# A graph layer's correction rows written into PSUM by ScalarE and accumulated onto by TensorE, in place of an addition on VectorE

## What is computed

```python
N_NODES = x.shape[0]
agg  = segment_sum(x[src], dst)              # sum of the neighbours' rows
deg  = segment_sum(ones, dst)
mean = agg / maximum(deg, 1)
h    = mean @ W_l + b + x @ W_r
y    = x + silu(h)
out  = (y - mean(y)) / sqrt(var(y) + 1e-5)   # along each row
```

## Time and profile before

| | us |
|---|---|
| median of 3 runs (1616.44 to 1617.76) | 1617.12 |
| the profiled execution's own time | 1616.76 |
| its span in the trace | 1615.0 |
| PE busy | 1574.8 (98%) |
| DVE busy | 1408.7 (87%) |
| ACT busy | 1028.8 (64%) |
| POOL busy | 947.9 (59%) |
| DMA, mean rate | 217 GB/s |

### The profile page before, as it was taken

How to read it: one execution, slowest core, us unless ns; L and a number is a source line. 1 busy time by engine, 2 the same in 40 slices (tenths; PEclk the granted TensorE clock), 3 DMA queues, 4 the chain that set the end, 5 groups by cost and what they waited for, 6 DMA issues and landing times.

```text
span 1615.0 us, 24709 instructions
## 1 busy us (share of the span) xinstructions
PE 1574.8 (98%) x7886; PEld 1311.1 (81%) x7886; DVE 1408.7 (87%) x2174; ACT 1028.8 (64%) x1433; POOL 947.9 (59%) x1089
## 2 busy tenths in 40 slices
PE   7998899999999999999999999999999999999996
PEld 5887688888888888888888888888888888888884
DVE  7988799999996888888888888888888888888886
ACT  4443343333335777777777777777777777777775
POOL 6446566666654665655566556665556656666563
PEclk9999999999999999999999999999999999999998
DMA  5456589888884676766667666666667666677674
GB/s 186 147 163 189 170 262 266 263 265 262 266 250 150 220 230 201 237 211 216 223 208 227 218 213 219 219 221 213 222 212 228 217 210 231 205 228 221 205 235 152
DMA packets 204245, 350.52 MB, mean 217 GB/s; under 512 B 37020, under 2 KB 51126, under 8 KB 204117
## 3 DMA queue, kind: packets, MB, share of 16 engines
q1 hardware_dynamic: 156135, 274.22, 51.6%
q0 software_dynamic: 46944, 74.22, 16.7%
q10 hardware_dynamic: 1038, 0.50, 0.1%
HBM read 288.78 MB, written 139.67 MB: 265 GB/s over the span
## 4 chain that ended last, share of the span: by engine, by line
PE 95%; DVE 2%; DMA 1%; issue 1%; SPq 0%; ACT 0%; POOL 0%; POOLq 0%; DVEq 0%
PE pH L473 81%; PE pT L567 9%; PE pT L541 3%; PE pT L482 1%; DMA light_h<-in_x 0%; DVE w_sum L799 0%; DVE w_sum L794 0%; DVE sums L923 0%; DMA light_x<-in_x 0%; PE pH L500 0%; PE pH L503 0%; DVE stats L1001 0%; SPq L246 0%; DVE row_mask L790 0%; DVE Z L794 0%
## 5 line engine op out<-in xcount | busy, mean ns | idle before, releaser
L473 PE MATMUL pH<-ws_hi,x_hi 128*128 128x512 f32 x1564 | 629.1, 402 | 0.0
L473 PE MATMUL pH<-ws_hi,x_lo 128*128 128x512 f32 x1564 | 611.4, 391 | 0.0
L473 PE MATMUL pH<-ws_lo,x_hi 128*128 128x512 f32 x1564 | 609.4, 390 | 0.0
L383 POOL DMA_INDIRECT cor<-correction_rows,node_idx x347 | 366.2, 1055 | 313.3 <-ACT cor L671 229.8
L708 ACT ACTIVATE x_hi<-pT 128x1024 fp32r<-128x1024 f32 x174 | 178.1, 1024 | 272.7 <-PE pT L567 272.7
L473 PEld LDWEIGHTS pH<-ws_hi,x_lo 128*128 128x128 f32 x1564 | 293.6, 188 | 63.3
L473 PEld LDWEIGHTS pH<-ws_lo,x_hi 128*128 128x128 f32 x1564 | 294.7, 188 | 54.5
L473 PEld LDWEIGHTS pH<-ws_hi,x_hi 128*128 128x128 f32 x1564 | 294.2, 188 | 54.5 <-issue 0.3
L986 DVE TENSOR_TENSOR Z<-pH,cor 128x1024 f32<-128x1024 f32 x174 | 212.5, 1221 | 100.4 <-PE pH L473 94.6
L717 ACT ACTIVATE O<-Z,shift,rstd 128x512 f32<-128x512 f32 x347 | 261.9, 804 | 3.2 <-DVE shift L1011 3.2
L1001 DVE BATCH_NORM_STATS2 stats<-Z 128x6 f32<-128x512 f32 x347 | 221.4, 680 | 0.0
(11 more groups left out here) (132 smaller groups left out, 1785.6 us busy)
## 6 DMA issues: line engine op xcount, KB each, us to landing
X<-in_x SPq DMA_DIRECT2D x173, 512.0 KB, 4.2
out<-O SPq DMA_DIRECT2D x173, 512.0 KB, 5.1
correction_rows<-c_out SPq DMA_DIRECT2D x98, 256.0 KB, 4.2
light_x<-in_x SPq DMA_DIRECT2D x66, 256.0 KB, 5.0
light_h<-early_product SPq DMA_DIRECT2D x44, 256.0 KB, 5.7
out<-light_o SPq DMA_DIRECT2D x44, 256.0 KB, 5.5
join_row<-joined SPq DMA_DIRECT2D x98, 64.0 KB, 4.1
light_h<-in_x SPq DMA_DIRECT2D x22, 256.0 KB, 2.9
```

The lines of the kernel that those rows point to most:

```text
L383: g.indirect_dma_start(out=out_, out_offset=None, in_=table, in_offset=bass.IndirectOffsetOnAxis(ap=idx, axis=0), bounds_check=bound, oob_ ...
L473: last = mm(ps, a[:, k], w[:, k], start=(n == 0), stop=(n == len(terms) - 1))
```

## The change

ACT gets a new step, `seed`: it copies the pair's correction rows `cor` into the two banks of `pH`. PE's matmuls of the pair wait for that (`seeded`) and accumulate from the first on, so `pH` holds the whole of h afterwards. Silu then reads `pH` and writes `Z`. `add_cor` on DVE and its semaphore are gone. ACT's order becomes silu t-1, `round_x` t+1, seed t+1, `reset_cor` t+3, light, normalise t-3. The reset of a third `cor` buffer joins the two in the edge stage, and POOL gathers for three pairs before `serve`, then for t+3 in turn t. One matmul more, written to the second bank of `pH[1]` after the edge tiles (`banks_open`), makes that bank ready for accumulation; its values are written over. For pairs 0 and 1 the seed waits for the last two edge tiles' `finish` and for `banks_open`, in place of PE's wait for `finish`.

```diff
--- before.py
+++ after.py
@@ -165,11 +165,12 @@
         c_stored = [sem(f"c_stored{b}") for b in range(2)]
         x_in = [sem(f"x_in{b}") for b in range(4)]
         cor_in = [sem(f"cor_in{b}") for b in range(4)]
-        transposed, hi_made, lo_made, product, z_made, silu_made = (sem("transposed"), sem("hi_made"), sem("lo_made"),
-                                                                   sem("product"), sem("z_made"), sem("silu_made"))
+        transposed, hi_made, lo_made, product, silu_made = (sem("transposed"), sem("hi_made"), sem("lo_made"),
+                                                                   sem("product"), sem("silu_made"))
         u_made, stats_made, mv_made, eps_added, rstd_made, shift_made, normed = (
             sem("u_made"), sem("stats_made"), sem("mv_made"), sem("eps_added"), sem("rstd_made"),
             sem("shift_made"), sem("normed"))
+        seeded, banks_open = sem("seeded"), sem("banks_open")
         cor_reset = sem("cor_reset")
         stored = [sem(f"stored{b}") for b in range(2)]
 
@@ -448,9 +449,10 @@
             gather_light(0)
             single(0, gather_cor)
             single(1, gather_cor)
+            single(2, gather_cor)
 
             def serve(t, q, u):
-                shifted(t, q, u, 2, NP, gather_cor)
+                shifted(t, q, u, 3, NP, gather_cor)
                 shifted(t, q, u, -2, NP, make_rstd)
                 light(q, u)
             peeled(0, NP, serve)
@@ -464,13 +466,14 @@
             mm = nc.tensor.matmul
             pe.wait_ge(consts, 5)
 
-            def three(ps, hi, lo, w_hi, w_lo, arriving=None):
+            def three(ps, hi, lo, w_hi, w_lo, arriving=None, seeded=False):
 
                 terms = [(a, w, k) for k in range(K) for a, w in ((hi, w_hi), (hi, w_lo), (lo, w_hi))]
                 for n, (a, w, k) in enumerate(terms):
                     if arriving and n % 3 == 0:
                         pe.wait_ge(arriving, k + 1)
-                    last = mm(ps, a[:, k], w[:, k], start=(n == 0), stop=(n == len(terms) - 1))
+                    last = mm(ps, a[:, k], w[:, k], start=(n == 0 and not seeded), stop=(n == len(terms) - 1),
+                              skip_group_check=seeded)
                 return last
 
 
@@ -581,6 +584,7 @@
 
 
             pe.wait_ge(early_kept, EARLY)
+            mm(pH[1][:, 1, :], s_hi[1][:, 0], wl_hi[:, 0], start=True, stop=True).then_inc(banks_open, 1)
 
             def node_pair(t, q, u):
                 shifted(t, q, u, 1, NP, transpose_x)
@@ -588,12 +592,10 @@
                 b = u % 2
                 wait(pe, hi_made, t + 1)
                 wait(pe, lo_made, t + 1)
-                if fixed(t) and t < 2:
-                    pe.wait_ge(c_made, ET - 1 + t)
-                wait(pe, z_made, t - 1)
+                pe.wait_ge(seeded, t + 1)
                 for a in range(nt):
                     last = three(pH[b][0:rows, a, :], x_hi[b][:, a, :, 0:rows], x_lo[b][:, a, :, 0:rows],
-                                 ws_hi, ws_lo)
+                                 ws_hi, ws_lo, seeded=True)
                 last.then_inc(product, 1)
             peeled(0, NP, node_pair)
 
@@ -667,7 +669,7 @@
 
             def reset_cor(t, q, u):
 
-                wait(act, z_made, t - 3)
+                wait(act, seeded, t - 3)
                 a_(cor[u][:], bias_rows[:].rearrange("p (a n) -> p a n", a=1).to_broadcast([P, 2, D]), ACT.Copy
                    ).then_inc(cor_reset, 1)
 
@@ -697,6 +699,7 @@
                     reset_light(0)
                     single(0, reset_cor)
                     single(1, reset_cor)
+                    single(2, reset_cor)
             peeled(0, ET, edge_tile)
 
 
@@ -718,11 +721,25 @@
                               bias=shift[0:rows, b, a:a + 1])
                 last.then_inc(normed, 1)
 
+            def seed(t, q, u):
+                nt, rows = pair_shape(t)
+                b, used = ring(q, u, 4)
+                wait(act, silu_made, t - 1)
+                if t < 2:
+                    act.wait_ge(c_made, ET - 1 + t)
+                    act.wait_ge(banks_open, 1)
+                if nt == 2:
+                    act.wait_ge(cor_in[b], 32 * (used + 1))
+                else:
+                    act.wait_ge(cor_in[b], 32 * used + 16)
+                a_(pH[u % 2][0:rows, 0:nt], cor[b][0:rows, 0:nt], ACT.Copy).then_inc(seeded, 1)
+
             def silu(t, q, u):
                 nt, rows = pair_shape(t)
                 b = u % 4
-                wait(act, z_made, t + 1)
-                a_(Z[0:rows, b, 0:nt], Z[0:rows, b, 0:nt], ACT.Silu).then_inc(silu_made, 1)
+                wait(act, product, t + 1)
+                wait(act, normed, t - 3)
+                a_(Z[0:rows, b, 0:nt], pH[u % 2][0:rows, 0:nt], ACT.Silu).then_inc(silu_made, 1)
 
             def light_make_silu(l):
                 wait(act, light_z, l + 1)
@@ -741,11 +758,13 @@
                     light_at(q + 1, reset_light)
 
             single(0, round_x)
+            single(0, seed)
 
             def node_pair(t, q, u):
-                shifted(t, q, u, 2, NP, reset_cor)
+                shifted(t, q, u, -1, NP, silu)
                 shifted(t, q, u, 1, NP, round_x)
-                shifted(t, q, u, -1, NP, silu)
+                shifted(t, q, u, 1, NP, seed)
+                shifted(t, q, u, 3, NP, reset_cor)
                 light(q, u)
                 shifted(t, q, u, -3, NP, normalise)
             peeled(0, NP, node_pair)
@@ -974,18 +993,6 @@
                                 pT[b][:, 0:nt].rearrange("p a (k r) -> p a k r", k=K)[:, :, :, 0:rows],
                                 x_hi[b][:, 0:nt, :, 0:rows].bitcast(f32), ALU.subtract).then_inc(lo_made, 1)
 
-            def add_cor(t, q, u):
-                nt, rows = pair_shape(t)
-                b, used = ring(q, u, 4)
-                wait(dve, product, t + 1)
-                if nt == 2:
-                    dve.wait_ge(cor_in[b], 32 * (used + 1))
-                else:
-                    dve.wait_ge(cor_in[b], 32 * used + 16)
-                wait(dve, normed, t - 3)
-                v.tensor_tensor(Z[0:rows, b, 0:nt], pH[u % 2][0:rows, 0:nt], cor[b][0:rows, 0:nt], ALU.add
-                                ).then_inc(z_made, 1)
-
             def residual(t, q, u):
                 nt, rows = pair_shape(t)
                 b = u % 4
@@ -1048,14 +1055,12 @@
             single(ET - 1, finish)
 
             def node_pair(t, q, u):
-                shifted(t, q, u, -1, NP, add_cor)
                 shifted(t, q, u, -2, NP, moments)
                 shifted(t, q, u, 1, NP, split_x)
                 shifted(t, q, u, -1, NP, residual)
                 shifted(t, q, u, -2, NP, make_shift)
                 light(q, u)
             peeled(0, NP, node_pair)
-            single(NP - 1, add_cor)
             single(NP - 2, moments)
             single(NP - 1, residual)
             single(NP - 2, make_shift)
```

## The result

The changed kernel takes 1629.33 us (median of 4 runs, 1628.76 to 1631.58) against 1616.78 us for the kernel before beside it: a ratio of **1.0079** (95% interval 1.0064 to 1.0094), 12.6 us slower. As a difference it was +8.7 us against +12.6: the direction, the place and the range held, the size was 3.9 us too small. The profiled execution has a span of 1627.9 us against 1615.0.

A forecast was written before the change was run, and what follows sets the result against it. PE was taken to bound the node stage at 6.34 us per pair; 0.95 + 9.4 + 1.4 - 3.1 = +8.7 us on 1616.76 gives 1625.4, 0.4 more for the median: 1625.8 us, range 1622.5 to 1632.

The forecast's parts named there:

- Part 1: Node stage, 173 full turns: DVE's lost addition gains 0, ACT's seed costs 0, smallest slack about 1.1 us.
- Rival A: Node stage: a wait returns through POOL's deviation or the load of X; half a microsecond 43 times, +21 us; chance 0.09.
- idle PE inside the node stage: Sign in the profile after that would show the prediction wrong and point to Rival A; no size given.
- Part 2: Edge stage's end: the third reset sits on a bare link and shifts all of it, +0.95 us (bounds 0.6 and 1.05).
- Part 3: Seam before pair 0: PE waits for the first seed, whose correction rows land late, +9.4 us (bounds 8.5 and 10.2).
- Part 4: After the seam's idle wait: PE restarts at half clock for about 3 us, +1.4 us (bounds 0 and 2.3).
- Part 5: Kernel's end: DVE's last additions leave its queue and the last moments come sooner, -3.1 us (bounds -1.1 and -3.9).
- 3.5 us set aside for matmuls that accumulate from the first on: First matmuls of 347 tiles: accumulating costs 0, upper bound 0.01 us each, 3.5 us in all.
- Rival B: PE's matmuls: a shorter step without DVE's traffic, 3.5 ns on about 4160 matmuls, giving 1611 us; chance 0.03.
- Rival C: Seam mostly hidden: gathers land 4 us sooner or PE finds work, clock stays; +2.5 us, 1619.6; chance 0.03.

The follow-up runs named there:

- e11: The changed kernel with 32 one-column fills more on POOL before its wait for the edge stores; one execution, 1629.50 us.
- e3: The changed kernel with the bank-opening matmul issued 36 times, inside PE's wait for the first seed; 1630.19 us, ratio to the kernel before 1.0066.
- e5: The changed kernel, but pairs 0 to 3 keep the addition on DVE and only later pairs are seeded; 1628.00 us, ratio to before 1.0073.
- e1: The changed kernel, but POOL makes t-2's reciprocal deviation before issuing the gathers of t+3; 1627.14 us, ratio to before 1.0048.
- e2: The changed kernel, but the third reset stands after the edge stage, in front of the first seed; 1629.85 us, ratio to before 1.0073.
- e4: The changed kernel, but POOL's gathers of pair 0 come before that of the light tile; 1632.41 us, ratio to before 1.0084.
- e7: The changed kernel with seeds only from pair 4 on, third reset after the edge stage, POOL's deviation before its gathers; 1614.56 us, ratio to before 0.9987.
- e9: As e7, but x is rounded before silu in turns whose silu waits for an addition; 1613.06 us, ratio to before 0.9980.
- e8: As e6, but third reset after the edge stage and x rounded before silu where silu waits for an addition; 1614.09 us, ratio to before 0.9989.
- e6: The changed kernel, but only pairs 168 to 173 seeded, others added on DVE, POOL's deviation before its gathers; 1718.81 us, ratio to before 1.0638.
- e10: The changed kernel, all pairs seeded, with the changes of e1 to e4 together; 1621.01 us, ratio to before 1.0034.

## Why the prediction was right, and where it fell short

*Part 1, node stage, cost 0.* The averages held: ACT 5.68 us per pair (predicted 5.70), the seed 1.03 (1.05), DVE 4.40. The first matmul's accumulating costs nothing: pairs are 6.34 us. What failed is "So cost 0, but with the smallest slack at about 1.1 us". The slack of a turn with light work was right (`x_lo` done at 596.2, PE's first matmul at 597.4), and it is eaten where POOL pauses: 2.14 us before the gather at 564.53. The trace of before has gaps of this kind too (3.79 us at 552.18, shown under e11), where gathers had turns to spare, and the step counted every gather at 1.30. The other slack of that step, 1.4 us for the load of X, was eaten too, by 0.2 us here, by 2.4 in e3 and by 2.7 in e5. Rival A was right in its mechanism, by both of its ways, and far off in its price: not half a microsecond in 43 turns, but 2.5 us in five. e1 shows the mechanism. By its own sign ("idle PE inside the node stage") the prediction was wrong in this part.

*Part 2, the third reset, 0.95.* Measured 0.94; e2 takes 1.00 away.

*Part 3, the wait, 9.4.* Measured 9.7: the landing came 0.2 us later than the row had it, the rest is below 0.1 (the signal to PE took 0.14). e4 moves one link of the chain and PE moves by it, e7 and e9 take the wait away.

*Part 4, the clock, 1.4, bounds 0 to 2.3.* The term that was mis-sized: "About 3 us at that level", taken from one earlier restart. Here the level lasted 5.7 us, and the cost was 2.6, above the upper bound of 2.3. Between the runs with this wait the level lasts from 3.8 to 5.7 us and costs from 1.7 to 2.6. That it is the clock and that the idle wait brings it is shown by e3.
By the Trainium skill's rule (TensorE: Matmul & The Clock Gate, Terms) half of the throttled time is lost: for 5.7 us an estimate of 2.8, against 2.6 measured: the trace agrees. The rule was not the error, the length put into it was.

*Part 5, the end, -3.1.* Measured -3.5: the moments of the last tile come 3.40 us after the last matmul's start (1618.21 less 1614.81; before 6.75). e8 shows that it comes from the last pairs alone. Beyond the moments the steps are the same up to the last normalise, 3.74 us against 3.73, as assumed; 0.15 more are behind that.

Of the 3.8 us missing in the profiles (12.46 against 8.65), 2.5 are part 1's long pairs, 1.2 the clock, 0.3 the wait, 0.2 small steps, less 0.4 at the end. PE's last matmul, forecast 11.8 us later, comes 15.95 later, counted from tile 94.

That the range held is in part luck. Parts 1 and 4 both fell outside their own bounds, and the room for them came from 3.5 us set aside for matmuls that accumulate from the first on, which cost nothing.

Rival B (a shorter matmul step) fell: pairs stay at 6.34 us with DVE at 171 of 200 us (e8) and at 139 (after). Rival C fell: the landing was where the row had it.

## To carry to other kernels

When a late addition is turned into an early seed, the operand is needed one whole product sooner: look first at the pair where that operand has only just come into being, and keep the old way for the first few. Taking work off an engine with cover all through gains only where the cover ends, here in the last pairs, and there a few seeded pairs do as much as all. After moving a step, follow each queue it was moved past, POOL's too: one line moved there took away all the long pairs, and the same line, in a build where an addition stood behind it, stood in the chain of most of a loss of 102 us (e6).

## What I had not expected of the hardware

POOL pauses before the same gathers in every trace, the 24th, 114th, 220th and 326th from `correction_rows`, for 1.1 to 4.4 us with nothing in the profile to release it (before: ahead of 552.18, 806.32, 1105.33 and 1403.49 us); it is no matter while gathers run turns ahead. That it goes by the number of gathers the traces show; what happens in the pause stays open. How long PE keeps the half clock after a restart was 3.1 us in one place of the kernel before and 3.8 to 5.7 at the seam of five runs, where pair 0 cost 1.7 to 2.6 us more. And the profiled position of one and the same edge tile lay 4 us apart in two runs of the same code up to there (489.01 in e1, 484.94 in e10, on another chip), more than most terms here, while e1 to e4, on one chip, lie within 0.4 us of each other: without a zero inside the kernel a single microsecond would not have shown.
